# Five signals of TensorE per edge group: raised by the last matmul, or by a drain behind it

## The reference

```python
h  = maximum(layernorm(x), 0)
p1 = tanh(h @ pp_W1 + pp_b1) @ pp_W2 + pp_b2
inter = concat([p1[src], p1[dst]]) @ pi_W1 + pi_b1      # per edge
inter = (inter @ pi_W2 + pi_b2) @ pi_W3                  # 64*8 values per edge
i1 = einsum('ecb,eb->ec', inter.reshape(E, 64, 8), edge_attr)
i1 = tanh(i1 @ ii_W1 + ii_b1) @ ii_W2 + ii_b2
x  = x + segment_sum(i1, dst)
```

## Time and profile before

| | |
|---|---|
| time without profiling, median of 3 runs | 1991.06 us (1988.24 to 1992.56) |
| the profiled execution, its own span | 2703.6 us |
| PE busy | 1947.7 us, 20012 matmul records |
| DVE / ACT / POOL busy | 1439.4 / 1089.0 / 1483.3 us |
| mean granted clock of PE | 0.852 |
| chain that ended last | PE 66%, issue 19%, unknown queue 8%, ACT 5% |

### The profile page before, as it was taken

How to read it: one execution, slowest core, us unless ns; L and a number is a source line. 1 busy time by engine, 2 the same in 40 slices (tenths; PEclk the granted TensorE clock), 3 DMA queues, 4 the chain that set the end, 5 groups by cost and what they waited for, 6 DMA issues and landing times.

```text
span 2703.6 us, 54970 instructions
## 1 busy us (share of the span) xinstructions
PE 1947.7 (72%) x20012; PEld 1270.4 (47%) x20012; DVE 1439.4 (53%) x1939; ACT 1089.0 (40%) x2419; POOL 1483.3 (55%) x1581
## 2 busy tenths in 40 slices
PE   4112987777777777777777777777777777787788
PEld 3101654444544544544445444455444444554556
DVE  4302875555555555555555555555555554555556
ACT  2211653434443343444444444444443343444344
POOL 4773025555655555665656566666655555555551
PEclk9555998888988888898988888988988788788889
DMA  4311222222221221222222222222222222222221
GB/s 86 80 28 31 58 46 43 44 45 42 50 49 39 48 47 41 51 50 43 50 46 45 49 49 45 49 48 45 50 46 45 44 46 43 44 44 42 42 42 45
DMA packets 261709, 127.00 MB, mean 47 GB/s; under 512 B 183561, under 2 KB 233720, under 8 KB 261448
## 3 DMA queue, kind: packets, MB, share of 16 engines
q1 hardware_dynamic: 209967, 74.11, 13.1%
q0 software_dynamic: 50048, 51.35, 10.4%
q10 hardware_dynamic: 1558, 0.15, 0.1%
HBM read 119.47 MB, written 6.00 MB: 46 GB/s over the span
## 4 chain that ended last, share of the span: by engine, by line
PE 66%; issue 19%; another core or an unknown queue 8%; ACT 5%; DVE 1%; DVEq 0%; ACTq 0%
PE bank L1337 34%; PE bank L1320 10%; PE bank L1344 7%; PE bank L1427 6%; PE spread_ps L1329 5%; PE bank L1304 3%; ACT tt_sb L702 2%; ACT st_sb L714 2%; PE bank L1352 0%; DVE o_sb L945 0%; PE spread_ps L1166 0%; ACT t_sb L705 0%; DVE acc_all L899 0%; DVE loc_bc L893 0%
## 5 line engine op out<-in xcount | busy, mean ns | idle before, releaser
L526 POOL DMA_INDIRECT u_rows<-u_tab,src_e x1436 | 1357.4, 945 | 1102.8 <-PE bank L1320 750.9
L1337 PE MATMUL bank<-o_sb,g_sb 128*64 128x256 f32 x6256 | 943.3, 453 | 153.2 <-issue 144.5
L945 DVE TENSOR_TENSOR o_sb<-st_sb,spread_ps 128x2048 f32<-128x2048 f32 x391 | 889.7, 2275 | 229.3 <-remote 111.3
L714 ACT ACTIVATE st_sb<-bank,s_bias 64x256 f32<-64x256 f32 x1564 | 733.1, 469 | 182.2 <-PE bank L1320 90.6
L1009 DVE TENSOR_TENSOR hot_t<-loc_bc,bank 126x512 bf16<-126x512 bf16 x391 | 268.4, 687 | 942.6 <-remote 615.3
L1337 PEld LDWEIGHTS bank<-o_sb,g_sb 128*64 128x64 f32 x6256 | 522.3, 162 | 434.7 <-issue 307.9
L702 ACT ACTIVATE tt_sb<-bank,z_bias 128x256 f32<-128x256 f32 x391 | 185.0, 473 | 706.1 <-PE bank L1337 364.4
L1344 PE MATMUL bank<-ident,tt_sb 128*128 128x128 f32 x782 | 183.3, 319 | 369.8 <-issue 211.1
L705 ACT COPY t_sb<-bank 128x256 f32<-128x256 f32 x391 | 146.1, 374 | 569.3 <-PE bank L1344 306.8
L1427 PEld LDWEIGHTS bank<-hot,t_sb 128*65 128x65 f32 x3128 | 224.4, 143 | 184.5 <-issue 182.1
L1427 PE MATMUL bank<-hot,t_sb 128*65 128x42 f32 x3128 | 274.5, 239 | 19.4 <-issue 18.6
(11 more groups left out here) (148 smaller groups left out, 361.9 us busy)
## 6 DMA issues: line engine op xcount, KB each, us to landing
loc_bc<-loc_tab SPq DMA_DIRECT2D x391, 126.0 KB
u_rows<-u_tab,src_e POOLq DMA_INDIRECT x1436
v_win<-v_tab SPq DMA_DIRECT2D x391, 15.8 KB
basis<-edge_attr SPq DMA_DIRECT2D x24, 256.0 KB
v_tab<-acc_all SPq DMA_DIRECT2D x6, 336.0 KB
basis<-u_tab,src_e POOLq DMA_INDIRECT x100
u_tab<-basis SPq DMA_DIRECT2D x6, 224.0 KB
x_sb<-x SPq DMA_DIRECT2D x1, 1120.0 KB
```

The source lines that it names most:

```text
L526: pool.indirect_dma_start(out=u_rows[:, g % UR, j, :] if g >= AHEAD else first_u[:, g - XG, j, :], out_offset=None, in_=u_tab[:, :], in_of ...
L714: last = nc.scalar.activation(tiles[h * D:(h + 1) * D, j], s_ps[part].rearrange("p (q a e) -> p q a e", q=2, a=TILES), ACT.Identity, bias= ...
L945: return nc.vector.tensor_tensor(o_sb[:, r, :, :].rearrange("p c (j e) -> p j c e", j=TILES), st_sb[:, r, :].rearrange("p (j e) -> p j e", ...
L1337: last = nc.tensor.matmul(z_ps[h * D:(h + 1) * D, 0:2 * P], g_sb[:, c, :], o_sb[:, r, c, 2 * h * P:(2 * h + 2) * P], start=(c == 0), stop= ...
```

## The change

In `step` each of the five `then_inc` on the last matmul of a part is replaced by a `drain` of TensorE behind that matmul, which raises the same semaphore by one. A drain is an instruction of the sequencer that ends when the engine has finished everything before it. The three forms of `newest` (made rows, first rows, ring rows) each get one, so every step has five drains. Nothing else is changed: the matmuls, the waits, the other engines and the counts are as before. The branch for inputs that aren't sorted tightly (`pe.Else`) keeps its signals on matmuls and doesn't run here.

```diff
                     elif g is not None:
                         pe.wait_ge(first_u_in[g - XG], 64)
-                        place_rows(first_u[:, g - XG, :, :], False).then_inc(s_ready, 1)
+                        place_rows(first_u[:, g - XG, :, :], False)
+                        pe.drain().then_inc(s_ready, 1)
                     else:
                         pe.wait_ge(u_in[u], n * (64 // UR) + (64 - AHEAD * (64 // UR)))
-                        place_rows(u_rows[:, u, :, :], False).then_inc(s_ready, 1)
+                        place_rows(u_rows[:, u, :, :], False)
+                        pe.drain().then_inc(s_ready, 1)
...
-                    spread_basis((u - 1) % BR).then_inc(spread_ready, 1)
+                    spread_basis((u - 1) % BR)
+                    pe.drain().then_inc(spread_ready, 1)
...
-                    z_group(u % 2).then_inc(z_ready, 1)
+                    z_group(u % 2)
+                    pe.drain().then_inc(z_ready, 1)
...
-                        last = nc.tensor.matmul(seg_ps, t_sb[:, (u - 3) % 2, j, :], hot[:, (u - 3) % HR, j, :],
+                        nc.tensor.matmul(seg_ps, t_sb[:, (u - 3) % 2, j, :], hot[:, (u - 3) % HR, j, :],
                                                 start=(j == 0), stop=(j == TILES - 1))
-                    last.then_inc(seg_ready, 1)
+                    pe.drain().then_inc(seg_ready, 1)
...
-                    t_transposes(u % 2).then_inc(t_ps_ready, 1)
+                    t_transposes(u % 2)
+                    pe.drain().then_inc(t_ps_ready, 1)
```

More of the change, by code:

```diff
@@ L1386, in newest @@
                         pe.wait_ge(rows_tanh, g // 2 + 1)
-                        place_made(g).then_inc(s_ready, 1)
+                        place_made(g)
+                        pe.drain().then_inc(s_ready, 1)
                     elif g is not None:
                         pe.wait_ge(first_u_in[g - XG], 64)
-                        place_rows(first_u[:, g - XG, :, :], False).then_inc(s_ready, 1)
+                        place_rows(first_u[:, g - XG, :, :], False)
+                        pe.drain().then_inc(s_ready, 1)
                     else:
                         pe.wait_ge(u_in[u], n * (64 // UR) + (64 - AHEAD * (64 // UR)))
-                        place_rows(u_rows[:, u, :, :], False).then_inc(s_ready, 1)
+                        place_rows(u_rows[:, u, :, :], False)
+                        pe.drain().then_inc(s_ready, 1)
                 turned_step = last_pass and n + u >= TURN
```

## The result

The changed kernel takes 2423.46 us (median of five runs, 2414.41 to 2466.18); the kernel before took 1991.06 beside it (1988.24 to 1993.82). The ratio is 1.2169, interval 1.2134 to 1.2205: slower by 432 us. The profiled execution is the longest of the five runs, with 2466.18 us at a span of 2464.4 and a mean granted clock of 0.891, and the ratio leaves it out; the others have clocks of 0.898 to 0.915.

What follows compares the result with a forecast made beforehand. GpSimd's gathers were taken as the bound, TensorE after the change: (a) 0.35, (b) 0.40, (c) 0.47, less (d) 0.05, make 1.17, a step of 5.27; 140 + 390 x 5.27 + 24 = 2219, predicted 2220 us, range 1996 to 2460.

Steps and rivals of the forecast that it cites:

- the slack behind the gathers: GpSimd's gathers take 4.86 us per group, TensorE's step 4.10; this 0.76 hides 228 of 457 us added to TensorE.
- The start S = 140 us: Assumed time of TensorE's first spread, from which the 390 step periods are counted.
- The burden of recording: Late matmul signals and stalls in the profiled execution, 712 us in all, taken as absent from runs without profiling.
- (a): At each change of parts on TensorE, the next weight load's overlap is lost: 0.07 us per drain, 0.35 per step.
- (b): The drain itself and the restart on TensorE: 0.08 us each, bounded between zero and 0.21.
- Dear drains: Rival: the restart behind each drain costs 0.2 us or more instead of 0.08, giving 2473 us; chance 0.07.
- (c): TensorE's sequencer work behind drains is uncovered: about 4.7 instructions per step at 0.10 us, 0.47 in all.
- (d): The transposes' stall for the tanh shrinks: 0.05 us less per step.
- The falling clock: Rival: holes behind drains lower TensorE's granted clock, adding 220 us for 2439; chance 0.11, shared with no slack.
- cheap drains: Rival: drains add under 0.6 us per step, hidden by GpSimd's 4.86 per group; 1991 to 2009 us, chance 0.14.
- late signals: Rival: matmul signals are partly late without profiling; prompt drain signals save 0.3 us per step, about 1875; chance 0.04.
- no slack: Rival: TensorE's steps already set the pace, so all 1.17 us per step counts, 2447; chance 0.11, shared with falling clock.

Runs made afterwards that it cites:

- the doubled drain: Changed kernel with a second drain ahead of each signalling drain, ten per step: 2808.62 us, ratio 1.41.
- the three gathers: Kernel before with three instead of four gathers per group, TensorE's instructions the same in number and size: 1710.02 us, ratio 0.8575.
- five drains, three gathers: Changed kernel with three instead of four gathers per group: 2424.68 us, ratio 1.2189.
- one filler: Changed kernel with one unused float32 matmul of 128 columns added per step ahead of `sum_v`: 2458.75 us, ratio 1.2339.
- 0.986 (two): Changed kernel with two unused float32 matmuls of 128 columns added per step ahead of `sum_v`: 2514.49 us, ratio 1.2654.
- waits ahead: Changed kernel with the waits of `z_group` and the segment sum moved ahead of the last matmul of the part before: 2208.26 us, ratio 1.1083.
- five fillers and drains: Changed kernel with five unused float32 matmuls of 128 columns added per step ahead of `sum_v`: 2757.66 us, ratio 1.3841.

## Why the prediction was right in direction and range, but short by nearly half of the loss

The sum gave 2220 us, 229 more than before; the loss is 432.

*TensorE becomes the bound, and the slack behind the gathers swallows part.* Right. Alone TensorE needed 1763 in the prediction and 1710 in the run; the slack was 228 there and 281 here.

*The start S = 140 us.* Wrong by 63: the first spread is at 76.8. It was read from a trace whose stretch between 135 and 256 us was itself stalled. The gathers' start was late with it (68.2 us in the earlier trace rows, 42.0 now), and so their pace had to come out as 4.86 us per group to meet the median, where 4 x 1.255 = 5.02 is measured. The 3% by which the account was off had been called near enough; they were the sign of the wrong start.

*The burden of recording.* The conclusion that the 712 us don't belong to the kernel was right, the reason was not: a second recording had none of it.

*Terms (a) and (b), 0.07 + 0.08 per drain.* Right. Behind the segment sum, and in most steps behind the placing, nothing but the drain stands, and the hole is 0.074. Behind the placing the load came 0.07 early before, which makes 0.15 in all as predicted (behind the segment sum it came only 0.03 early, for the tanh's sake), and the doubled drain gives 0.074 for (b) alone. The drain rows of VectorE and of TensorE's end were a good guide. Dear drains fall. The 2407 that the prediction worked out beside its sum lies near the median by luck: it takes a step of 5.75 us, where 5.52 is measured, and no loss by the clock.

*Term (c), 0.47 for 4.7 instructions at 0.10.* The mechanism is right, shown by moving the waits; the size is short. The holes exceed 0.074 by 0.065, 0.157, 0.142, 0 and 0.278, which is 0.64: a single wait costs 0.13 (0.208 - 0.074 in most steps behind the spread), the two instructions behind the transposes 0.22, and the end of a loop pass 0.72. The largest hole stands behind the transposes as forecast, the next behind the spread and not behind `z_group`. *Term (d)* holds: the tanh ends at 1004.48, the transposes load at 1004.90. By the holes the step grew by 1.30 (before they sum to -0.29), by the full-clock steps by 5.52 - 4.15 = 1.37, where 1.17 was predicted.

*The falling clock.* This was a rival with 0.11 and its place in the likeliest case was nothing. It is real: 216 us of the profiled execution, 177 of a run near the median. The step that failed is the argument "the holes will be 0.2 us, not the 2.2 of rows 3": short holes, five in each step, let the clock fall as well. The rival's own size was good, 220 us, and its sum, 2439, lies within the runs. The Trainium skill's page TensorE: Matmul & The Clock Gate, section A second HAM failure mode: psum-queue depth-cycling, tells of a kernel whose clock swung because TensorE idled briefly and often between groups of matmuls; the trace agrees, with five holes of 0.07 to 0.35 us in the mean in each step and 122 stretches at 1.2 GHz. It had been open to the prediction. The Trainium skill prices the time at 1.2 GHz at one half of it on the same page, section HAM oscillation — how this bites in real kernels; here it was 0.43.

The sum, mended term by term: 2220, less 63 for S, plus 390 x (5.52 - 5.27) = 97 for the step (0.20 of it from (c) and the loop's ends, 0.05 because the step before is 4.15 and not 4.10 in the mean), less 6 for the end, is 2248; with 216 for the clock it is the span of 2464. For a run near the median, 2248 + 177 = 2425. The errors in S and in the step nearly cancelled, which is luck; what parts 2220 from the median of 2423 is mostly the clock. The own range of the likeliest case, to 2350, missed; the whole range, to 2460, held only because it made room for the rivals. The last of the checks named in advance, a time over 2400 with a period near 5.3, was said to speak against the slack. It came true and the slack was right: the check had left out the clock.

The cheap drains (time under 2009) and the late signals fall with the result. The floor, *no slack*, falls with the three gathers.

## What to carry to other kernels

A drain of TensorE costs little itself. It costs the overlap with the next part, and it exposes every wait and every register operation that the sequencer would have worked off ahead. If a drain must stay, the waits for what comes behind it belong ahead of the last matmul in front of it, where they are fulfilled by then. Work out a hole's price twice, at the full clock and with the clock that the holes may cost. And where an account of two engines' paces is off by some per cent, look at where each starts before calling it near enough.

## What the runs showed of the hardware that was not expected

- The granted clock doesn't follow the busy share of TensorE's rows alone: three kernels with PE busy 81% had 0.909 (five drains, three gathers), 0.962 (one filler) and 0.986 (two), and one with 84% had 0.958 (waits ahead) where one with 83% had 0.993 (five fillers and drains). What decides it is not settled by these runs.
- One execution of the kernel before had matmul signals two microseconds late for most of its length; the second had none.
- GpSimd's gathers keep 1.25 us each through all 1536 of them in the second trace of before, while TensorE's clock is at either level; once TensorE had caught up with them, they were the pace of the kernel before.
